# Four closing operations of 1024 columns, each written as four of 256

## What is computed

```
        dst = jnp.einsum('bhij,bhje->bhie', attention, h) + bias[None, :, None, :]
        out = jax.nn.relu(dst) + h
        mu = out.mean(axis=-1, keepdims=True)
        var = out.var(axis=-1, keepdims=True)
        out = (out - mu) / jnp.sqrt(var + EPS) * ln_gamma[None, :, None, :] + ln_beta[None, :, None, :]
...
    x = _layernorm(x + _L1_gnn_ref(x, adj, ...), axis=-1)
```

## Time and profile before

| | us |
|---|---|
| median of three runs | 4538.3 |
| lowest and highest run | 4529.56 and 4540.33 |
| the profiled execution | 4534.18 |
| its span, from the first to the last instruction | 4532.4 |
| busy: DVE | 3907.6 (86%) |
| busy: PE | 3262.6 (72%) |
| busy: POOL | 3097.0 (68%) |
| busy: ACT | 2166.3 (48%) |

### The profile page before, as it was taken

How to read it: one execution, slowest core, us unless ns; L and a number is a source line. 1 busy time by engine, 2 the same in 40 slices (tenths; PEclk the granted TensorE clock), 3 DMA queues, 4 the chain that set the end, 5 groups by cost and what they waited for, 6 DMA issues and landing times.

```text
span 4532.4 us, 57997 instructions
## 1 busy us (share of the span) xinstructions
PE 3262.6 (72%) x13058; PEld 1490.9 (33%) x13058; DVE 3907.6 (86%) x10912; ACT 2166.3 (48%) x4674; POOL 3097.0 (68%) x3204
## 2 busy tenths in 40 slices
PE   2333377777777787877777777778777777787996
PEld 1222233333333333333333333333333333333332
DVE  6555588999989999999999999999899899998776
ACT  4343444555545555555555455555444555453222
POOL 5777777777777777777777777777777777776000
PEclk8555588888888888888988888888888888888998
DMA  5444444545454545445545454455545445543001
GB/s 159 150 150 144 152 143 146 167 153 168 144 166 153 166 150 166 152 151 157 166 154 157 157 164 156 143 166 155 164 149 166 153 152 159 167 154 119 28 19 33
DMA packets 264132, 659.03 MB, mean 145 GB/s; under 512 B 62002, under 2 KB 128691, under 8 KB 247475
## 3 DMA queue, kind: packets, MB, share of 16 engines
q0 software_dynamic: 153600, 419.64, 31.6%
q1 hardware_dynamic: 110258, 236.60, 14.8%
HBM read 605.67 MB, written 50.33 MB: 145 GB/s over the span
## 4 chain that ended last, share of the span: by engine, by line
DVE 31%; DMA 25%; issue 20%; PE 15%; POOL 6%; ACT 3%; DVEq 1%; POOLq 0%; SPq 0%; ACTq 0%
DMA rows<-in_x_dram,idx 24%; PE acc L1291 11%; DVE uv L856 8%; DVE peak L888 8%; POOL rows L517 6%; DVE top L755 3%; DVE key_b L757 1%; PE pB L1248 1%; ACT maskT L570 1%; DVE key_a L757 1%; DVE agg L895 1%; DVE agg L888 1%; DVE sth L935 1%; DVE key_b L770 1%; PE pT L1186 1%
## 5 line engine op out<-in xcount | busy, mean ns | idle before, releaser
L517 POOL DMA_INDIRECT rows<-in_x_dram,idx x3200 | 3096.8, 968 | 1081.1 <-DMA rows<-in_x_dram,idx 934.9
L1291 PE MATMUL acc<-uv,hs 128*65 128x512 f32 x4096 | 2113.0, 662 | 312.6 <-DVE uv L856 312.3
L856 DVE SCALAR_TENSOR_TENSOR uv<-rq,qinv,maskT 128x512 f32<-128x512 f32 x2048 | 1463.2, 737 | 61.2 <-PE rq L1220 48.1
L888 DVE TENSOR_TENSOR peak<-peak,rows 128x512 f32<-128x512 f32 x1408 | 967.0, 687 | 277.6 <-DMA rows<-in_x_dram,idx 268.4
L1291 PEld LDWEIGHTS acc<-uv,hs 128*65 128x65 f32 x4096 | 576.4, 153 | 1514.0 <-issue 1094.8
L1235 PE MATMUL pA<-id,xt 128*128 128x128 f32 x256 | 81.9, 420 | 819.2 <-DVE agg L899 819.2
L659 ACT ACTIVATE xaT<-pA 128x512 f32<-128x512 f32 x128 | 76.4, 597 | 881.3 <-PE pA L1235 875.9
L566 ACT ACTIVATE stage<-pT 128x1024 bf16<-128x1024 f16 x256 | 263.1, 1028 | 443.3 <-PE pT L1186 359.0
L540 ACT ACTIVATE mask_sb<-adj_sb 128x2048 f16<-128x2048 int32 x128 | 243.9, 1905 | 212.1 <-DMA adj_sb<-in_adj_dram 211.9
L1235 PEld LDWEIGHTS pA<-id,xt 128*128 128x128 f32 x256 | 35.3, 194 | 919.4 <-DVE agg L899 498.6
L1248 PE MATMUL pB<-w_sb,xaT 128*128 128x256 f32 x1024 | 270.6, 412 | 12.5 <-ACT xaT L659 12.5
(11 more groups left out here) (114 smaller groups left out, 3700.5 us busy)
## 6 DMA issues: line engine op xcount, KB each, us to landing
adj_sb<-in_adj_dram SPq DMA_DIRECT2D x128, 1024.0 KB, 6.7
rows<-in_x_dram,idx POOLq DMA_INDIRECT x3200
xh_dram<-xh SPq DMA_DIRECT2D x128, 256.0 KB, 2.4
xr<-xh_dram SPq DMA_DIRECT2D x64, 512.0 KB, 4.2
xt<-in_x_dram SPq DMA_DIRECT2D x128, 128.0 KB, 6.6
out_dram<-xr SPq DMA_DIRECT2D x32, 512.0 KB, 4.0
w_sb<-in_L_gnn_W_dram SPq DMA_DIRECT2D x1, 512.0 KB
wcat<-in_L_gnn_W_dram SPq DMA_DIRECT2D x2, 128.0 KB
```

The source lines that it names most:

```text
L517: nc.gpsimd.indirect_dma_start(rows[:, k * C:(k + 1) * C], None, x_rows, bass.IndirectOffsetOnAxis(ap=idx[u][:, k:k + 1], axis=0), engine_ ...
L856: stt = nc.vector.scalar_tensor_tensor(uv[k][:, i, :], rq[:], inv, m, ALU.max, ALU.mult)
L888: top_of = nc.vector.tensor_tensor(into, peak[:, 0:n], new, ALU.max)
L1291: last = nc.tensor.matmul(acc[h % 2][0:HW, :], hs[:, past(quad, u) + jt, h, :], uv[k][:, i, :], start=(jt == 0), stop=(jt == JT - 1))
```

## The change

The four operations of a quad's closing that worked on 1024 columns at once are each issued as four operations of 256 columns, one behind the other, one for each of the quad's tiles. The last of each four carries the semaphore that the one operation carried. The operands, the arithmetic, the places in the order and all waits stay. The helper that repeated gamma and beta over four tiles goes, since each operation of 256 columns reads them as they are.

```
-                    nc.vector.tensor_tensor(dst[:], raw[:], xr[:], ALU.add).then_inc(s_fin, 1)
+                    for i in range(QT):
+                        last = nc.vector.tensor_tensor(dst[:, i, :], raw[:, i, :], xr[:, i, :], ALU.add)
+                    last.then_inc(s_fin, 1)
...
-                    nc.vector.tensor_tensor(dst[:], dst[:], per_column(gamma_b), ALU.mult).then_inc(s_fin, 1)
+                    for i in range(QT):
+                        last = nc.vector.tensor_tensor(dst[:, i, :], dst[:, i, :], gamma_b[:], ALU.mult)
+                    last.then_inc(s_fin, 1)
...
-                    nc.vector.tensor_tensor(dst[:], dst[:], per_column(beta_b), ALU.add).then_inc(s_fin, 1)
+                    for i in range(QT):
+                        last = nc.vector.tensor_tensor(dst[:, i, :], dst[:, i, :], beta_b[:], ALU.add)
+                    last.then_inc(s_fin, 1)
...
-                    nc.vector.tensor_tensor(dst[:], dst[:], xr[:], ALU.add).then_inc(s_fin, 1)
+                    for i in range(QT):
+                        last = nc.vector.tensor_tensor(dst[:, i, :], dst[:, i, :], xr[:, i, :], ALU.add)
+                    last.then_inc(s_fin, 1)
```

More of the change, by code:

```diff
@@ L913, in per_head @@
                 return a.unsqueeze(2).to_broadcast([P, QT * HEADS, HO])
-            def per_column(a):
-                return a[:].unsqueeze(1).to_broadcast([P, QT, C])
             def finish_heads(quad, part):
```

## The result

The changed kernel takes 4546.3 us (median of 16 runs, 4543.1 to 4551.4), the kernel before 4536.3 us on the same chips (16 runs, 4529.6 to 4540.3). The ratio is 1.0022 with a 95% interval of 1.0015 to 1.0029: 10.0 us slower, which is 0.22%. The forecast was 22 us more; the time lies inside the range and near its lower edge.

What follows compares the result with a forecast made beforehand. No engine bounds alone: VectorE paces 14 of 25 quads, gathers 11. 11.8 + 9.2 = 21 us, plus 2.7 behind the gathers, is 23.7, less a little: 22 us more, 4560 us forecast, range 4540 to 4578.

Steps and rivals of the forecast that it cites:

- Length of four narrow operations: On VectorE, four operations of 256 columns take 1.40 us, 0.20 more than a wide one; 21 us in the coupled part.
- The rival of operations that do not overlap: On VectorE, each narrow operation costs 0.424 us, 0.49 us more per wide one: 4595 us; chance 0.08.
- Held to the last part: On GpSimd, a gather started under four narrow operations waits for the last: 0.8 us a quad, 21 us over 26 quads.
- the upper case: At beta (L975), the gather is stretched by 0.5 us if L786 behind it holds too, else 0.2; 0.35 taken.
- The residual's sum: At L981, which already holds a gather for nearly its whole length, the hold grows by 0.1 us a quad.
- the gathers' term: On GpSimd, longer holds add 21 us to the gathers, of which 9.2 us count in 11 of 25 quads.
- the first rival: Held gathers get in between narrow operations, GpSimd's stream 39 us shorter: 4531 to 4546, about 4540 us; chance 0.2.
- What of VectorE's length counts: VectorE sets the pace in 14 of 25 quads, so 11.8 of its 21 us count there.
- the second rival: Slack in VectorE's and GpSimd's idle time takes up the added length; a third remains, 4546 us; chance 0.12.
- Behind the last gather: After the last gather, 23 operations add 4.6 us on VectorE, of which 2.7 us count.
- the likeliest case: Whole kernel: both streams lengthen and held gathers wait to the last part, 4560 us, own range 4552 to 4572; chance 0.6.

Runs made afterwards that it cites:

- residual's sum alone: Kernel before with only the residual's sum divided into four, the other three operations wide: 4525.8 us, ratio 0.9977.
- the three others: Kernel before with the sum, gamma and beta divided into four, the residual's sum wide: 4550.6 us, ratio 1.0034.
- two memsets ahead, wide: Kernel before, all four operations wide, with two memsets of 48 columns ahead of each: 4535.6 us, ratio 1.0001.
- one memset ahead, narrow: Changed kernel with a one-column memset ahead of the four parts of sum, gamma and beta: 4521.3 us, 0.9970 of the kernel before.
- one memset ahead, wide: Kernel before with a one-column memset ahead of the wide sum, gamma and beta: 4529.0 us, ratio 0.9986.
- length alone: Kernel before with extra one-input statistics on VectorE, results unused, placed where no gather is held: 4542.0 us, ratio 1.0014.
- other places: Changed kernel with the closing's first two places (`FINISH_AT`) moved from 11 and 12 to 14 and 15: 4521.3 us, 0.9973 of the kernel before.
- other places and memset: Changed kernel with places 14 and 15 and the memset ahead of three of the divided operations: 4508.2 us, 0.9939 of the kernel before.

## Why the prediction was right or wrong, point by point

**Length of four narrow operations: right.** 1.40 was taken from L986; 1.40 to 1.43 us was measured, 0.21 us more than a wide one where 0.20 was used. In the coupled part that is 22 us instead of 21. The rival of operations that do not overlap is out.

**Held to the last part: right at three places.** All 77 gathers under the sum, gamma and beta are held past the last part and the next instruction. The sum and gamma together grew by 45.4 - 35.6 = 9.8 us, 0.38 a quad (0.35 forecast); beta by 13.2 us, 0.5 a quad, the full price that L786 was given as the upper case (0.35 taken). The prediction's "all 54 gathers that were held by L928 or L971" are 52 of 53. Gathers under other instructions, for which it had no term, were held 5.9 us longer.

**The residual's sum: wrong.** The step "L981 holds for nearly its whole length already, and gets from -0.1 to +0.2: 0.1" measured 4.6 - 23.4 = -18.8 us, -0.72 a quad. The prediction took one kind of hold from the rows of L971 and L784 and put it on L981 too. The row of L981 could not tell which kind it was, since the instruction behind it (L755) has one input: the gather at 2522.41 would end 0.83 us behind L981 either way. And its own rows had shown both kinds, for the gather at 2516.14 went on ahead of L786. What the runs showed in its place: a gather under the residual's four parts gets in at the end of the part that runs, 26 of 26. A memset ahead of the operation in VectorE's program goes with that, and kernels with a memset put ahead of the other operations moved the difference with it. So the gathers' term was +9.8 us, not +21. This is the first rival's mechanism at one of four places. At all four places, by the memset, it gave 13.1 us faster than before, beyond the bound of 7 us faster in that rival, which had only VectorE's waits for rows to win from; the gathers' own shorter stream was what there was to win.

**What of VectorE's length counts: too high.** The step "In the 14 of 25 quads where VectorE sets the pace, its 21 us count" gave a share of 0.56. With the gathers nearly unchanged the share was 7.6 / 32.2 = 0.24 (0.07 to 0.32 by the interval). In the change itself it was about nothing beyond the holds: GpSimd's other time in 25 quads stayed at 828 us. A quad in which VectorE does not wait for rows is not yet one in which it sets the pace. By these runs the gathers set it in the kernel before over the 25 quads taken together, and VectorE began to only when they got shorter. This is nearest to the second rival, that the slack takes up two thirds, which had idle time in general for its ground.

**Behind the last gather:** 3.4 us, where 2.7 were forecast: right.

The 25 quads of each profiled execution, as differences from the kernel before (us; the measured time is the difference of the medians of the whole):

| kernel | gathers | GpSimd's other time | 25 quads | measured |
|---|---|---|---|---|
| the change | +9.7 | -0.7 | +9.0 | +10.0 |
| residual's sum alone | -21.8 | +15.0 | -6.8 | -9.9 |
| the three others | +14.0 | -0.4 | +13.6 | +15.0 |
| two memsets ahead, wide | -0.6 | -0.4 | -1.1 | 0.0 |
| one memset ahead, narrow | -41.1 | +28.1 | -13.0 | -13.1 |
| one memset ahead, wide | -9.3 | +0.2 | -9.1 | -5.3 |
| length alone | +3.1 | +1.2 | +4.3 | +7.6 |
| other places | -25.8 | -0.3 | -26.1 | -14.4 |
| other places and memset | -40.3 | -0.3 | -40.5 | -26.2 |

Where GpSimd's other time stays, the quads get longer or shorter by what the gathers do. It rises by more than 1.2 us in only two kernels, both with shorter gathers and the old places. With other places, where VectorE's wait for the root is gone, it does not, but the part behind the last gather gets 15 to 18 us longer.

For the size of the error, put the measured values into the prediction's own sum. The gathers' 9.8 us in place of 21, at its shares, give 22 x 0.56 + 9.8 x 0.44 = 16.6 us in the coupled part instead of 21. With the gathers' share at one they give 9.8, and with the 3.4 us behind them 13.2, against 12.6 in the spans of the profiled executions. So the hold at the residual's sum made some 4 us of the error and the share some 7; had the gathers' term been 21 as forecast, the share would not have mattered. The measured time lies inside the stated range and below the likeliest case's own (4552 to 4572): it was the rivals that had set the range's lower part.

The Trainium skill, page SBUF — State Buffer, § Who interferes with whom, states that a VectorE instruction with two SBUF inputs contends with a GpSimd instruction that reads SBUF, and that the pair of ports they share is locked for a whole instruction. By that rule short instructions let a gather in sooner. The rows of L985, and of the narrow operations behind a memset, agree; those of L926, L971 and L977 in the changed kernel don't, and there the measurement decides.

**Open:** why what stands ahead changes when a held gather gets in. The runs show that a memset does it, of one and of 48 columns, ahead of narrow and of wide operations, and that behind masked products most gathers get in too (22 of 29), but not what in the engine does it. No run has another small instruction in the memset's place. Nor is it shown why 9 gathers go against the sorting by what stood ahead, or why 25 under beta before the change went on ahead of L786: in the kernel with the residual's sum alone, 10 of 22 gathers that began at the same distance from the end of L975 were held to the end of L786.

## What to carry to other kernels

Where GpSimd issues gathers beside VectorE's work with two inputs in SBUF, price such work by what stands ahead of it and behind it, not by its length alone: here a split by itself kept the gathers out for longer (+10 us), and with one tiny memset ahead it let them in (-13 us). When rows show two kinds of hold, don't put the one on all places, least of all on one whose row can't tell them apart. And when two streams meet now and then, split a long stretch into the busy time and the other time of each stream before giving either a share: the one whose other time stays the same when the other engine gets longer is the one that sets the pace.

## What the hardware showed that was not expected

- A gather that is held by VectorE ends 0.81 to 0.83 us behind the end of the instruction that lets it go, and which one that is goes with what ran ahead. Behind a maximum, or behind the statistics' aggregate ahead of beta, it was the last of an unbroken row of two-input instructions (77 of 77 after, 52 of 52 under the sum and gamma with L784 behind them before). Behind a memset it was the one that ran (26 of 26 in the residual's sum after, 46 of 46 with wide operations behind two memsets), and behind masked products one before the last in 22 of 29. The kernel before has exceptions to the first: 25 gathers that began 0.14 to 0.15 us before the end of beta went on ahead of the L786 that followed.
- Four operations of 128x256 with two inputs in SBUF take 1.40 to 1.43 us back to back, with starts 0.33 us apart, against 0.42 us for one and 1.21 us for 128x1024.
- Two memsets of 48 columns took 0.15 us together by the records, and added 0.10 us to VectorE's busy time at each place in the mean (12.9 us at 128 places); 96 memsets of one column added nothing that the page shows (3937.3 against 3937.8 us).
